# One block for the state-space part and attention, and routing done chunk by chunk into lists in DRAM

## The reference

```python
x = x + mamba(layernorm(x))                       # depthwise conv, selective scan, gate; 512 channels, 16 states
x = x + cross_attention(layernorm(x), ctx, ctx, pos)  # 16 heads of 16, 77 context rows per sequence, rotary on q
x = x + moe(layernorm(x))
# selective scan
dA = exp(delta[..., None] * A);  BX = delta[..., None] * Bm * xc[..., None]
h[t] = dA[t] * h[t-1] + BX[t];   y = sum_n h * C + D * xc;   out = (y * silu(z)) @ out_w.T
# moe: 8 experts, width 1024, top 2
probs = softmax(x @ gate_w.T);  topw, sel = top_k(probs, 2);  topw = topw / sum(topw)
out = sum_e combine[:, e] * ((up_e * gelu(gate_e)) @ down_w[e].T)
```

## Time and profile before

| | us |
|---|---|
| median of 3 runs | 2112.5 (2111.75 to 2113.33) |
| profiled execution | 2112.57 |
| its span | 2110.8 |
| PE busy in the span | 1893.8 (90%) |
| DVE busy | 1172.5 (56%) |
| ACT busy | 1087.4 (52%) |
| POOL busy | 1044.1 (49%) |

### The profile page before, as it was taken

The page is one execution under the profiler, slowest core; times in us unless marked ns, Lnnn a source line. Parts: engine busy times, 40 slices in busy tenths (PEclk is TensorE's granted clock), DMA queues, the critical chain, the costliest instruction groups (busy, mean ns, idle before and its releaser), DMA issues. The chain is left out here.

```text
span 2110.8 us, 29062 instructions
## 1 busy us (share of the span) xinstructions
PE 1893.8 (90%) x10714; PEld 1536.7 (73%) x10714; DVE 1172.5 (56%) x1664; ACT 1087.4 (52%) x2119; POOL 1044.1 (49%) x712
## 2 busy tenths in 40 slices
PE   6889999999999998848999983799999999999998
PEld 2667777777777777736666653688888888888887
DVE  4889898989898988826666546311111111111111
ACT  3898989898989898715666650111111111111111
POOL 1687888788878787706646521222222222222121
PEclk8999999999999999969999995999999999999999
DMA  4021211111211111040000018444444444444441
GB/s 123 26 61 41 61 51 61 51 61 51 61 51 61 41 61 41 21 110 28 21 31 31 31 40 301 173 117 133 114 136 113 137 112 137 112 138 111 134 148 18
DMA packets 86637, 176.81 MB, mean 84 GB/s; under 512 B 12593, under 2 KB 57137, under 8 KB 76258
## 3 DMA queue, kind: packets, MB, share of 16 engines
q1 hardware_dynamic: 72834, 156.27, 21.6%
q0 software_dynamic: 13664, 18.69, 5.4%
HBM read 152.52 MB, written 22.41 MB: 83 GB/s over the span
## 5 line engine op out<-in xcount | busy, mean ns | idle before, releaser
L238 POOL TENSOR_TENSOR m_hc_ring<-m_h_ring,m_c_bc 128x1024 f32<-128x1024 f32 x256 | 605.8, 2372 | 122.4 <-DVE m_h_ring L399 104.1
L1559 PE MATMUL e_ps<-e_xT,w 128*128 128x256 f32 (+1 forms) x2560 | 503.1, 358 | 0.8 <-ACT e_xT L1486 0.8
L1559 PEld LDWEIGHTS e_ps<-e_xT,w 128*128 128x128 f32 x2560 | 443.0, 192 | 51.3 <-issue 1.1
L1470 POOL DMA_INDIRECT out<-e_y,ids x71 | 113.3, 1595 | 565.3 <-DVE e_y L1522 480.1
L490 PEld LDWEIGHTS m_ps<-m_ident,m_bxT 128*128 128x128 f32 x2048 | 234.6, 141 | 210.8 <-DVE m_h_ring L399 96.9
L283 ACT ACTIVATE m_a_ring<-m_delta,m_negA 128x512 f32<-128x512 f32 x512 | 366.3, 716 | 39.6 <-DVE m_h_ring L399 39.2
L490 PE MATMUL m_ps<-m_ident,m_bxT 128*128 128x128 f32 x2048 | 320.4, 279 | 61.9 <-DVE m_h_ring L399 55.9
L295 ACT ACTIVATE m_bxT<-m_uT,m_bT 128x512 f32<-128x512 f32 x512 | 364.7, 713 | 0.0
L1513 DVE TENSOR_TENSOR e_hT<-e_gact,e_ps 128x512 f32<-128x512 f32 x142 | 97.6, 687 | 447.4 <-ACT e_gact L1495 447.4
L399 DVE TENSOR_TENSOR_SCAN m_h_ring<-m_a_ring,m_carry,m_ps 128x512 f32<-128x512 f32 x256 | 316.2, 1265 | 27.5 <-ACT m_a_ring L283 13.5
L399 DVE TENSOR_TENSOR_SCAN m_h_ring<-m_a_ring,m_ps 128x512 f32<-128x512 f32 x256 | 303.6, 1207 | 35.8 <-ACT m_a_ring L283 12.4
(11 more groups left out here) (201 smaller groups left out, 2009.1 us busy)
## 6 DMA issues: line engine op xcount, KB each, us to landing
w<-in_gate_up_w SPq DMA_DIRECT2D x80, 1024.0 KB, 6.8
m_c_bc<-c_rows SPq DMA_DIRECT2D x32, 1024.0 KB, 5.9
w<-in_down_w SPq DMA_DIRECT2D x8, 1024.0 KB, 11.8
m_x_in<-in_x SPq DMA_DIRECT2D x8, 512.0 KB, 5.3
m_x_res<-in_x SPq DMA_DIRECT2D x8, 512.0 KB, 6.5
x<-m_x_res SPq DMA_DIRECT2D x8, 512.0 KB, 2.8
t_xa<-x SPq DMA_DIRECT2D x8, 512.0 KB, 4.0
out<-t_xa SPq DMA_DIRECT2D x8, 512.0 KB, 2.9
```

The source lines that it names most:

```text
L238: p.tensor_tensor(hc_ring[:, k % HC, :, :], h_ring[:, n % 2, e:e + 2, :], c_bc[:, n, :].unsqueeze(1).to_broadcast([P, 2, CT]), ALU.mult).t ...
L1470: nc.gpsimd.indirect_dma_start(out=out, out_offset=bass.IndirectOffsetOnAxis(ap=ids[:, tile:tile + 1], axis=0), in_=y[:, s % 2, i, :], in_ ...
L1559: last = t.matmul(gu_bank(s, g, which)[:, f * wide:(f + 1) * wide], w1[:, s % W1_RING, c, lo:lo + P], xT[:, s % 2, c, 0:wide], start=(c == ...
```

## The change

**One block for two parts.** The state-space part and attention become one block. All their tiles lie in one arena with offsets from two tables: `STATE_MAP` lists the state-space tiles, and `ATTENTION_MAP` puts the attention tiles under state-space tiles that are dead by the end. `attention_parts` now returns the programs, and `ATTEND_AT` says behind which slot of the state-space part each prologue slot g goes. SP starts `load_constants` one chunk before the end. Attention's eight tiles of x, one per chunk, become a ring of 5 that is refilled as tiles come free. Keys and values of the prologue use one PSUM bank in turn.

**Routing per chunk.** `dispatch_phase` is gone. Two chunks behind the steps, DVE chooses the experts from the logits (`choose` in slots 4 and 5, 14 small operations), PE ranks them (job RK at the end of slot 7), DVE computes shares and list positions (`share_out` and `place`, 9 small operations in slot 7), and POOL writes records (token, weight) into a list in DRAM with 8 indirect DMAs (`scatter`, slot 0 of chunk c+3). The step table is made at the end on DVE (`list_steps`).

**Experts.** The weights are loaded in the experts' block. SP loads for each step its records (`load_meta`, at an address read from the table), POOL copies the token numbers and gathers as before with a ring of 4, so the gather of step s+3 is issued before the scatter of step s. In `down` PE loads a second register, the count for its wait on the down matrix.

```diff
+ATTEND_AT = {(-1, 60): range(-16, -9), (0, 0): (-9,), (0, 6): (-8,), (0, 21): (-7,), (0, 22): (-6,), (0, 23): (-5,),
+             (0, 24): (-4,), (0, 51): (-3,), (0, 53): (-2,), (0, 55): (-1,)}
...
-        def slots(body):
+        def slots(body, attend):
             for h in range(-2, NCH + 1):
                 for s in range(STEPS):
                     body(h, s, STEPS * h + s, 0 <= h + 1 < NCH, 0 <= h < NCH, h - 1 >= 0)
+                    for g in ATTEND_AT.get((h - NCH, s), ()):
+                        attend(g)
+            for g in range(0, parts.last):
+                attend(g)
...
+                if h == NCH - 1:
+                    sp.wait_ge(z_done, TI * NCH)
+                    sp.wait_ge(ut_done, KE * NCH)
+                    sp.wait_ge(dt_done, KE * NCH)
+                    sp.wait_ge(a_ready, STEPS * (NCH - 1))
+                    sp.wait_ge(bxT_ready, STEPS * (NCH - 1))
+                    sp.wait_ge(x1_stored, 16 * 2)
+                    parts.load_constants(sp)
...
+    jobs_at = [[("XT", 0, 1), ("XT", 1, 1)], [("Q", 0, 1)], [("Q", 1, 1), ("NT", 0, -2)], [("NT", 1, -2)],
+               [("LG", 0, -2)], [("OUT", 0, -1)], [("OUT", 1, -1), ("QT", 0, 1)],
+               [("QT", 1, 1), ("RK", 0, -2)]]
...
+        def scatter(c):
+            pool.wait_ge(placed, c + 1)
+            if c == 0:
+                pool.wait_ge(blanked, 16 * 3)
+            for k in range(2):
+                for i in range(TI):
+                    nc.gpsimd.indirect_dma_start(
+                        out=slots, out_offset=bass.IndirectOffsetOnAxis(ap=pos_u[:, c % 2, k, i:i + 1], axis=0),
+                        in_=rec[:, c * TI + i, k, :], in_offset=None).then_inc(scattered[c % 2], 16)
...
+            if q in (4, 5) and 0 <= c - 2 < NC:
+                choose(c - 2, q - 4)
+            if q == 7 and 0 <= c - 2 < NC:
+                share_out(c - 2)
+                place(c - 2)
...
+            if kind == "RK":
+                pe.wait_ge(chosen, c + 1)
+                flat = upto[:].rearrange("p e i -> p (e i)")
+                t.matmul(job_bank[:, 0:E * TI], rank_w[:, 1, :], flat, start=True, stop=False)
+                t.matmul(job_bank[:, 0:E * TI], rank_w[:, 0, :], both[:].rearrange("p e i -> p (e i)"),
+                         start=False, stop=True)
+                t.matmul(job_bank[:, E * TI:E * TI + E], rank_w[:, 1, :], upto[:, :, TI - 1],
+                         start=True, stop=True).then_inc(rk_done, 1)
...
-    X_RING = 3
+    X_RING, M_RING, M_AHEAD = 4, 8, 4
...
+            for s in range(STEPS):
+                if s >= W1_RING:
+                    sp.wait_ge(gu_done, first_group[s - W1_RING + 1])
                 load_w1(sp, s, tables, gate_up_w, w1, w1_loaded)
+                if s == 0:
+                    for r in range(M_AHEAD):
+                        load_meta(r)
+                if s < E:
+                    if s:
+                        sp.wait_ge(w2_loaded, 16 * s)
+                    sp.dma_start(w2[:, s, :, :], down_w[s].rearrange("(c p) d -> p c d", p=P)).then_inc(w2_loaded, 16)
+                if s + M_AHEAD < STEPS:
+                    load_meta(s + M_AHEAD)
...
+                pool.wait_ge(meta_loaded[s % M_RING], 16 * (s // M_RING + 1))
+                lo, n = tiles_of[s][0], len(tiles_of[s])
+                nc.gpsimd.tensor_copy(who[:, lo:lo + n], meta[:, lo:lo + n, 0]).then_inc(who_ready, 1)
...
-                e = pe.value_load(tables[0:1, s:s + 1], min_val=0, max_val=E - 1)
-                if s == 0:
-                    pe.wait_ge(w2_loaded, 16 * E)
+                e = pe.value_load(tables[0:1, 0, s:s + 1], min_val=0, max_val=E - 1)
+                pe.wait_ge(w2_loaded, pe.value_load(tables[0:1, 2, s:s + 1], min_val=16, max_val=16 * E))
```

1441 lines of the change are left out of this document (714 added, 727 removed).

## The result

| | before | after |
|---|---|---|
| median, us | 2112.1 (2110.9 to 2113.3, 4 runs) | 2095.7 (2093.1 to 2098.6, 4 runs) |
| profiled execution, us | 2112.6 | 2098.6 |
| its span, us | 2110.8 | 2096.8 |

The ratio is 0.9921, 95% interval 0.9910 to 0.9933. The change makes the kernel 16 us faster, where 50 were forecast. The direction was right, the time at the very edge of the range, the size a third of what the sum gave.

What follows compares the result with a forecast made beforehand. The prediction took long stretches as back-to-back PE work, with gains at the joins. From a span of 2110.8, -37 + 20 - 28 - 5 gave 2060.8, with 1.8 outside the span 2062.6; forecast 2062.5 us, range 2038 to 2096.

Steps and rivals of the forecast that it cites:

- Part 1: Join of state space and attention in one block: second maximum ends at 934, not 970.42; -37 us.
- with the output projection's rest in between I take 9.4: Attention's start: 9.4 us from last rotation's end to second maximum's end, against 8.5 in the old trace.
- Part 2: Steady attention, eight chunks: routing work on DVE and store bursts on POOL add 20 us.
- so two slots, 9.1 us, hide a burst: 1 us stays, six times: POOL, slot 0: normalise is needed three steps later, covering most of a 10.1 us burst; 5 us taken.
- The DVE terms: Attention: nine operations before apply in slot 7 cost 12 us; fourteen in slots 4 and 5 cost 3.
- Part 3: Last logits to first expert transpose: PE starts at 1311.5, not 1339.70; -28 us.
- The low end: Start of experts: -16 us if gathers land 7 us behind weight loads or SP's register loads are dearer.
- Part 4: Inside the experts: ring of 4 removes the 3.31 us gather wait and 1.6 us slower gate-up; -5 us.
- (a): Rival: POOL becomes attention's bound, with store bursts of 15 us; +25, total 2088 us; chance 0.22.
- (b): Rival: attention's store bursts and DVE operations are absorbed; 16 us less, total 2046 us; chance 0.12.
- (c): Rival: second register load in the experts shows on PE, 56 us; total 2118 us, slower; chance 0.07.
- (d): Rival: joins don't shorten, prologue slow on DVE or gathers behind weight loads; 17 us less won, 2080; chance 0.05.

Runs made afterwards that it cites:

- e1: The changed kernel without the record stores of chunks 0 to 6 and the waits on them; 2066.2 us.
- e9: The kernel of e1 with slot 7's DVE order changed: rank bank read, apply, then the other seven small operations; 2067.4 us.
- e6: The changed kernel with the records of the first four steps loaded before the first gate-up matrix on SP; 2090.7 us.
- e11: As e3, but SP loads the record of step 0 ahead of the first gate-up matrix, the other three behind it; 2072.8 us.
- e3: The changed kernel with the early chunks' record stores spread, one in each of the 8 slots; 2077.4 us.
- e8: The kernel before the change with X_RING 4 for 3 and nothing else; 2107.8 us, ratio 0.9981.
- e2: The changed kernel with the early chunks' record stores spread, two each in slots 0, 2, 6 and 7; 2079.3 us.
- e10: The changed kernel with the burst of eight stores kept whole but in slot 6, not slot 0, for all but the last chunk; 2085.2 us.
- e5: The changed kernel, still one block, with all 16 slots of attention's prologue behind the last state-space slot; 2117.0 us.

## Why the prediction was right in direction and wrong in size

**Part 1 (-37 forecast, -27.1).** The first steps of the sum held. These rows of the changed kernel answer to the earlier trace rows:

```profile
892.20 3.82 DVE L479 TENSOR_TENSOR_SCAN m_h_ring<-m_a_ring,m_carry,m_ps 128x512 f32<-128x512 f32 x3
895.94 3.63 DVE L1076 TENSOR_SCALAR t_xn<-t_xa,t_mv,t_rstd 128x256 f32<-128x256 f32 x4
900.19 2.48 DVE L524 TENSOR_TENSOR m_zT<-m_ps,m_zT 128x512 f32<-128x512 f32 x4 [0.61 <-PE m_ps L587]
...
915.68 0.69 DVE L1210 TENSOR_TENSOR t_q<-m_ps,t_bq 128x512 f32<-128x512 f32 x1 [1.49 <-PE m_ps L1290]
...
923.32 1.27 POOL L911 TENSOR_TENSOR t_q_rot<-t_rope_a,t_rope_b 128x512 f32<-128x512 f32 x1
...
937.15 0.69 DVE L554 TENSOR_TENSOR m_x_res<-m_ps,m_x_res 128x512 f32<-128x512 f32 x1 [0.61 <-PE m_ps L678]
...
937.90 1.30 PE L1335 MATMUL m_ps<-t_k_blk,t_qT 128*128 128x308 f32 x4 [0.78 <-DVE m_x_res L554]
...
939.24 0.80 DVE L1091 TENSOR_REDUCE t_nmax<-m_ps 128x8 f32<-128x616 f32 x1 [1.40 <-PE m_ps L1335]
```

Scans end at 896.0 (895.5 forecast), the query copy at 916.4 (916.6), the rotation at 924.6 (924.6). The step that failed is the next: "with the output projection's rest in between I take 9.4" us to the second maximum. It took 15.4. The second scores need a bank that the residual sum (L554, 937.15) frees, and PE had value matmuls and 32 projection matmuls to make in order. The next steps run slower too (starts of the maxima 6.8, 5.0 and 4.5 us apart, against 2.0, 3.3 and 3.3), since the rest of the values stands among them; that takes 3 us more up to the first bias addition. PE is busy 14.3 of the 15.4 us (924.6 to 940.0), against 6.9 of the 8.5 us that the sum took as its model (961.9 to 970.4 before): in the new prologue PE itself is the pace.

**Part 2 (+20 forecast, +43.8).** The price of a store was right (1.28 us, 1.27 forecast). The step that failed is "so two slots, 9.1 us, hide a burst: 1 us stays, six times". The stores cost 27.2 us and not the 5 to 8 that the sum left. The first wait came as the terms say: with masking ahead 10.1 + 3 - 9.1 = 4.0, and DVE waited 4.15 us in the burst shown. But the sum let the matter end there. POOL has only 2.0 us of idle time a slot by the earlier trace rows, and less than that in slots 1 and 3 to 5, and so all that stands there comes late as well. DVE, ACT and PE each keep their order, so that one late reciprocal holds back the next maximum and what follows it. PE's idle time grew by 13.5 us. The second thing is a term that the sum didn't have: the same matmuls took 13.7 us longer, at a granted clock of 0.92 against 0.97 in e1. This is half of what the stores cost.

The DVE terms came out in size, 16.6 us without stores against 12 + 3 and the 1.7 of Part 3, and that is in part luck. Their mechanism, PE waiting for an `apply` that nine operations delay by 2 us, did not hold: PE waits 1.05 us there, e9 shows that the order makes no difference, and 0.7 us a chunk are the rank matmuls on PE. Of the 16.6 us, 10.3 lie in the five chunks between the third and the eighth bias addition and 6.2 behind them; no run takes the latter apart.

The forecast named a sign of being wrong, chunks with a burst of over 42 us. It came true: of the five intervals listed under e1, four have 43.3 to 47.2 us. The other sign, a longer stretch of experts, did not (766.1 us).

**Part 3 (-28 forecast, -25.3).** From the last logits to the first expert transpose 35.1 us were forecast and 39.7 measured, so it is off by 4.6 us; the 2.7 of the totals are smaller because of the 1.7 us named under the result. Burst, landing and register loads came as summed: the first records were issued 24.5 us after the logits, 24.4 in the forecast. From there it took 6.4 us to the copy, where 4.8 had been taken, and from the end of the second gather 6.1 us to PE's start, where 2.8 had been taken. The low end named that case ("as late as 7 us behind the weight loads"), and e6 and e11 show it: with records or the first record ahead of the weights, PE starts 10 us earlier than in the changed kernel (e6) and 6.5 us earlier than in e3 (e11). One thing stays open. From the last store's end to SP's first issue it takes 6.6 us in the changed kernel, e6 and e11, and 3.0 in e1, with the same last eight stores.

**Part 4 (-5 forecast, -5.0).** e8, with the ring alone, shows it (4.5 us by the medians, 4.9 in the stretch of the experts). The second register load costs nothing: pair steps have the same 13.8, 6.9 and 0.44 us, and the chain goes from piece to piece without a gap:

```profile
1338.58 13.82 PE e_ps L1584 x64
1352.40 6.91 PE e_ps L1597 x32
1359.31 0.44 PE e_ps L1571 x4
...
1993.98 0.22 PE e_ps L1571 x2
1994.20 7.15 PE e_ps L1584 x64
```

**The rivals.** (a) POOL as attention's bound came nearest in time (2088, measured 2095.7), but not by its mechanism: stores did not take 1.9 us beside a busy DVE, and e2, e3, e10 have as much POOL work and 10 to 18 us less time. In the section of the Trainium skill that the prediction names, page "SBUF — State Buffer", section "🔬 SBUF: two separate sides", it is some DVE operations that keep GpSimd from writing descriptors. Beside DVE's sums, maxima, additions and `apply` a store still took 1.28 us, so the trace doesn't show it here; which of them the page's rule covers, no run tells. (b) and (c) did not occur. (d) came true in good part: by the stage table the two joins gave 9.9 and 2.7 us less than their terms, where (d) has 17. Its gathers behind weight loads occurred; its prologue was slow by PE's work and not by DVE's. So the miss is made of Part 2 (23.8 us) and the joins (12.6), and the rival that names the joins had a chance of 0.05. The chances were too firm on the sum: 0.54 for a forecast that hung on one subtraction, a burst less two slots.

## What to carry to other kernels

The idle time of an engine is cover for an added piece only where it lies behind that piece, and before anything that others wait for: walk through the next five or six operations on that engine and see which ends late, instead of subtracting whole slots from the piece. Then read PE's busy time over equal work as well as its idle time: half of what the stores cost here was slower matmuls. Spread added DMA issues over many slots, or put them ahead of the slots with the least work; against e1, the same stores cost 29.5 us in slot 0, 19 in slot 6 (e10), and 11 to 13 when spread (e3, e2). A join between stages gains from work that runs during the old stage's tail, and less from earlier loads (e5), until the engine that carries both becomes the pace.
